# Zero products on TensorE ahead of the first weights, and another order of the first tiles' steps, in a graph attention layer with a spline network

## The reference

```python
HW = h @ W
s = HW @ a[:OUT_F, 0]
t = HW @ a[OUT_F:, 0]
e = jax.nn.leaky_relu(s[row] + t[col], negative_slope=ALPHA)
m = jax.ops.segment_max(e, row, num_segments=N_NODES)
ex = jnp.exp(e - m[row])
den = jax.ops.segment_sum(ex, row, num_segments=N_NODES)
agg = jax.ops.segment_sum((ex / den[row])[:, None] * h[col], row, num_segments=N_NODES)
basis = _b_splines(agg, _grid())
out = jax.nn.silu(agg) @ base_w.T + jnp.einsum('nip,oip->no', basis, spline_w)
return _layernorm(x + out, axis=-1)
```

## Time and profile before

| | before |
|---|---|
| median of 3 runs | 412.33 us |
| the profiled execution | 412.93 us |
| its span, first to last instruction | 411.1 us |
| TensorE busy | 378.2 us (92%) |
| VectorE busy | 353.7 us (86%) |
| ScalarE busy | 261.5 us (64%) |
| mean granted TensorE clock | 0.973 |

### The profile page before, as it was taken

How to read it: one execution, slowest core, us unless ns; L and a number is a source line. 1 busy time by engine, 2 the same in 40 slices (tenths; PEclk the granted TensorE clock), 3 DMA queues, 4 the chain that set the end, 5 groups by cost and what they waited for, 6 DMA issues and landing times.

```text
span 411.1 us, 5022 instructions
## 1 busy us (share of the span) xinstructions
PE 378.2 (92%) x1850; PEld 295.6 (72%) x1850; DVE 353.7 (86%) x442; ACT 261.5 (64%) x264; POOL 32.8 (8%) x108
## 2 busy tenths in 40 slices
PE   5997615999999999899999999999999999999993
PEld 2545404888888888778788888788777777777782
DVE  7999959977887587999899999989799959999645
ACT  2758427465665697886587686496476677678212
POOL 5100001000000000010101010101010010101000
PEclk9999865999999999999999999999999999999999
DMA  7996826000000009545364545442524164563202
GB/s 258 385 236 20 28 17 206 0 2 0 0 2 0 2 4 348 183 123 186 107 200 139 169 129 178 121 136 56 150 53 102 51 176 158 135 192 83 71 18 105
DMA packets 23882, 46.54 MB, mean 113 GB/s; under 512 B 1878, under 2 KB 2218, under 8 KB 23858
## 3 DMA queue, kind: packets, MB, share of 16 engines
q1 hardware_dynamic: 12770, 24.78, 22.9%
q0 software_dynamic: 11088, 21.44, 19.2%
HBM read 43.02 MB, written 2.56 MB: 111 GB/s over the span
## 4 chain that ended last, share of the span: by engine, by line
PE 50%; issue 31%; DVE 11%; POOL 4%; DMA 2%; DVEq 1%; ACT 0%; POOLq 0%
PE PS L1165 25%; PE PS L1121 17%; POOL wh L410 3%; DVE oh L419 3%; PE PS L1104 3%; DMA wh<-in_splT 2%; PE PS L1067 2%; DVE still L433 2%; PE PS L1131 1%; PE PS L1032 1%; DVE xl L442 1%; DVE wl L642 1%; PE PS L1053 0%; DVE ex L678 0%; DVE scrap L650 0%
## 5 line engine op out<-in xcount | busy, mean ns | idle before, releaser
L1165 PE MATMUL PS<-wh,s 128*128 128x512 f32 (+1 forms) x720 | 225.3, 392 | 2.2 <-DVE wl L642 1.0
L1165 PEld LDWEIGHTS PS<-wh,s 128*128 128x128 f32 (+1 forms) x720 | 133.4, 185 | 36.5 <-ACT s L935 3.7
L1165 PE MATMUL PS<-wl,s 128*128 128x512 f32 (+1 forms) x360 | 141.1, 392 | 0.0
L935 ACT ACTIVATE s<-v 128x1280 fp32r<-128x1280 f32 (+1 forms) x32 | 40.0, 1252 | 63.9 <-DVE v L750 59.4
L1165 PEld LDWEIGHTS PS<-wl,s 128*128 128x128 f32 (+1 forms) x360 | 66.7, 185 | 15.2
L744 DVE SCALAR_TENSOR_TENSOR v<-v,v 128x1280 f32<-128x1280 f32 (+1 forms) x32 | 46.5, 1454 | 4.8 <-ACT v L921 4.8
L750 DVE SCALAR_TENSOR_TENSOR v<-v,v 128x1280 f32<-128x1280 f32 (+1 forms) x32 | 46.7, 1461 | 3.3
L760 DVE SCALAR_TENSOR_TENSOR s<-v,s 128x1280 fp32r<-128x1280 f32 (+1 forms) x32 | 46.5, 1454 | 0.2 <-ACT s L935 0.2
L746 DVE SCALAR_TENSOR_TENSOR v<-v,v 128x1280 f32<-128x1280 f32 (+1 forms) x32 | 46.5, 1454 | 0.0
L918 ACT ACTIVATE v<-xt,bias 128x1280 f32<-128x1280 f32 (+1 forms) x32 | 42.9, 1342 | 3.5 <-DVE s L760 2.1
L410 POOL DMA_DIRECT2D wh<-in_splT x32 | 22.9, 714 | 279.1 <-PE PS L1165 164.2
(11 more groups left out here) (133 smaller groups left out, 353.4 us busy)
## 6 DMA issues: line engine op xcount, KB each, us to landing
wh<-in_splT POOLq DMA_DIRECT2D x32, 512.0 KB, 4.8
wring<-in_splT SPq DMA_DIRECT2D x21, 512.0 KB, 4.3
xt<-in_xT SPq DMA_DIRECT2D x1, 2500.0 KB, 11.6
xn<-in_x SPq DMA_DIRECT2D x1, 2304.0 KB
xh<-in_x POOLq DMA_DIRECT2D x1, 2304.0 KB, 13.3
out<-xr SPq DMA_DIRECT2D x9, 256.0 KB
wh<-in_baseT POOLq DMA_DIRECT2D x4, 512.0 KB, 4.8
wring<-in_baseT SPq DMA_DIRECT2D x3, 512.0 KB, 4.2
```

The costliest lines, as they stand in the source:

```text
L935: e.activation(parts(sh, u), bufs(u)[0], ACT.Relu).then_inc(s_shi, 1)
L1165: m = e.matmul(PS[0:rows(w), w % 8, :], sx[:, ic, tl * 128:tl * 128 + rows(w)], wx[:, ic, :], start=first and n == 0, stop=last and n == 2)
```

## The change

`keep_warm(n)` issues `n` products of a zero matrix with 500 zero columns into PSUM bank 6, and nothing reads them. Eight stand ahead of the loop over the remaining edges, six behind it, eight more behind a wait for `greatest(0)`, four behind `e1(0, 0)`, four behind `e2(0, 0)`; then comes the first transpose. The order of steps for tiles 0 to 3 changes on VectorE, ScalarE and TensorE.

```diff
@@ vector
             greatest(0)
             small(0)
             greatest(1)
+            weigh(0, 0)
             small(1)
-            weigh(0, 0)
             weigh(0, 1)
-            inverse(0)
             p_low(0, 0)
+            weigh(1)
             greatest(2)
             small(2)
             p_low(0, 1)
-            weigh(1)
+            inverse(0)
             inverse(1)
+            greatest(3)
+            p_low(1)
             weigh(2)
             inverse(2)
-            p_low(1)
-            greatest(3)
             small(3)
             greatest(4)
             small(4)
@@ scalar
             for p in range(2):
                 e1(0, p)
                 e2(0, p)
+            p_high(0, 0)
             e1(1)
-            p_high(0, 0)
+            e2(1)
             p_high(0, 1)
-            e2(1)
             e1(2)
+            p_high(1)
             e2(2)
-            p_high(1)
             normalise(0)
             e1(3)
-            e2(3)
             for j in range(1, NT - 1):
...
                 p_high(j + 1)
+                if j == 1:
+                    e2(3)
@@ tensor
+            def keep_warm(n):
+                for k in range(n):
+                    e.matmul(PS[:, 6, 0:CW], nought[:, 0:128], nought[:, :], start=True, stop=True)
+
             e.wait_ge(s_scol, 3)
+            keep_warm(8)
             with e.Fori(0, left) as n:
...
-            def aggregate(j, i0=0, i1=3):
-                if j >= 2 and i0 == 0:
+            def aggregate(j, products):
+                end = 1 if j == 0 else 2
+                if j >= 2 and 0 in products:
                     e.wait_ge(s_ya, j - 1)
-                for i in range(i0, i1):
+                for i in products:
...
-                    if j <= 1 and i == 2:
+                    if j == 0 and i == 2:
                         e.wait_ge(s_xlo, NT)
...
+            keep_warm(6)
+            e.wait_ge(s_tmax, 1)
+            keep_warm(8)
+            e.wait_ge(s_e1, 1)
+            keep_warm(4)
+            e.wait_ge(s_e2, 1)
+            keep_warm(4)
             turn(0, 0)
             turn(0, 1)
-            for j in range(NT):
-                aggregate(j, 0, 2)
+            aggregate(0, (0, 2))
+            turn(1)
+            aggregate(0, (1,))
+            for j in range(1, NT):
+                aggregate(j, (0, 1))
                 if j + 1 < NT:
                     turn(j + 1)
-                aggregate(j, 2, 3)
-                if j:
-                    back(j - 1)
+                aggregate(j, (2,))
+                back(j - 1)
```

More of the change, by code:

```diff
@@ L1121, in aggregate @@
                         m = e.matmul(PS[:, 5 + j % 2, :], pp[0:r, j % 3, place(j, t), :], xs[0:r, t, :],
-                                     start=(i == 0 and t == 0), stop=(i == 2 and t == NT - 1))
-                if i1 == 3:
+                                     start=(i == 0 and t == 0), stop=(i == end and t == NT - 1))
+                if end in products:
                     m.then_inc(s_agg, 1)
```

## The result

Over 17 runs of each the changed kernel takes 413.33 us against 412.14 us: a ratio of 1.0029 (95% interval 1.0019 to 1.0039). The runs spread more, 412.04 to 414.94 us against 411.56 to 412.7 us. Forecast was 412.1 us and no change; the range 411.0 to 413.5 us holds the time, the direction is wrong. Ratios leave out an execution that is over 1.5% above the fastest of its kernel; the only one in this document is the 421.98 us of `after_256`.

A forecast was written before the change was run, and what follows sets the result against it. VectorE's and ScalarE's queues, not TensorE's clock, were taken as the bound. -0.55 (new order) + 0.2 (first eight) + 0.05 (clock) = -0.3, taken as -0.25: 412.33 - 0.25 = 412.1 us, range 411.0 to 413.5.

The forecast's parts named there:

- `weigh(1)` behind `e2(1)`: VectorE's `weigh(1)` waits for ScalarE's `e2(1)` and starts near 68.9 us, which hides `p_low(0, 0)`.
- the gap in `turn(1)` and its releaser: TensorE waits almost 1 us before the ninth transpose of `turn(1)`, until VectorE's L701, `p_low(0, 1)`, is done.
- the last group of tile 0: TensorE's last products of tile 0 start near 75.2 us, where before they started at 75.55.
- the gain there: Attention stage: 0.55 us gained, 0.2 lost to the first eight and 0.05 to the clock: 0.3, taken as 0.25.
- the first eight: Zero products ahead of the loop's product L1089: at half clock they end at 57.95 and make it 0.2 us late.
- the prediction's own bound: The eight at full clock take 1.7 us, end by 56.3, cost nothing; a faster L1089 gives back up to 0.2.
- the sixteen: Zero products behind `greatest(0)`: 3.4 us at full clock, over by 64.7, not holding up the first transpose.
- the 0.1 that the prediction had weighed: If transposes don't count as busy, the clock is lost before tile 0's 20 products; the gain is 0.1 us smaller.
- So 0.55 is kept, and the stage goes on as before: Tile 0's last group starts at 75.0 instead of 75.55 us; later steps of tiles 1 to 3 keep that lead.
- its signs of being wrong: `turn(0, 0)` coming after 65.5 us, no gap in `turn(1)`, or TensorE waiting anew at `turn(2)`.
- the rivals: TensorE bounded after all, 411.0 us, chance 0.17; zero products in the way; first eight at upper bound, 413.7 us, 0.03.
- the slower one: Sixteen zero products before `turn(0, 0)`, half of them at half clock: +1.2 us, 413.5 us; chance 0.23 in all.

The follow-up runs named there:

- `after_256`: Changed kernel plus 196 do-nothing TensorE instructions (satisfied waits) in the first stage and around the loop: 418.0 us, ratio 1.0138 to the kernel before.
- `zeros_only`: Kernel before, in its own order of steps, with the 30 zero products added: 413.49 us, ratio 1.0031.
- `early_low`: Changed kernel with seven zero products ahead of the loop, earlier `p_low(0, 1)` and `p_high(1)`, and 198 satisfied waits in tiles 2 to 8: 411.74 us, ratio 0.9986.
- the changed kernel plus 196: Changed kernel with 196 do-nothing TensorE instructions (satisfied waits) spread over the products of tiles 2 to 8: 412.0 us, ratio 0.9994 to the kernel before.
- 30 waits: Kernel before with 30 satisfied waits on TensorE spread over products: 412.99 us, ratio 1.002.
- 120: Kernel before with 120 satisfied waits on TensorE spread over the products of tiles 2 to 6: 412.48 us, ratio 1.0006.

## Why the prediction was wrong

Right, by its own steps: where the bound stood (VectorE's queue, not the clock; `zeros_only` shows it for the old order), `weigh(1)` behind `e2(1)` (68.9 said, 68.91 measured), the gap in `turn(1)` and its releaser (almost 1 us said, 0.76 by the sum, 0.90 measured), the last group of tile 0 (75.2 said, 75.20 measured), the gain there (0.25 to 0.3 said, 0.36 measured).

Right in number alone, and so by luck: the first eight, with 0.2 us taken and 0.26 measured. At half clock they were to hold the loop's product until 57.95. In fact the clock fell at 55.3 us, with four of them under way at full clock; they ended at 57.22, TensorE idled 0.71 us, and VectorE's operand was there at 57.54, as before (57.52). In `zeros_only` the eight ran at full clock, were over at 56.4, and the product still came 0.30 us late, where the prediction's own bound had no delay. Between the start of L618 and that product lie 0.47 us in the kernel before and in `early_low` with seven, 0.71 and 0.72 in the changed kernel and `zeros_only`, 0.57 in the changed kernel plus 196. What holds it up is open.

Missed, at little cost: the clock was to be back before 61 us and came at 62.2, after two of the sixteen had run at half. The last of them started at 64.91 us and the first transpose's load of weights at 65.02, released by VectorE's L681 at 64.97; so they held it up by 0.1 us at most. Nor does the clock stay for certain: it lasted in the profiles of the changed kernel and `zeros_only`, and was at 0.50 again from 67.3 to 70.7 us in the changed kernel plus 196 and from 68.3 to 71.7 in `early_low`. There `turn(2)` started at 82.06 (plus 196) against 81.97 us: the 0.1 that the prediction had weighed.

Wrong is the sentence in which the sum was closed, "So 0.55 is kept, and the stage goes on as before", with its counterpart "from 80 us on everything as before, 0.3 us earlier". It priced the added products as work in an idle stretch and left out that they are 60 instructions in a stream that is fetched in blocks. None of its signs of being wrong could show it, since all of them end by 82 us. The omitted term is a fetch one unit earlier: in the profiled execution 1.6 us of idle time near 204 us; by medians 1.2 us over the kernel before, or 1.5 us over the changed kernel's own attention stage. Removing it by moving the fetch a whole period (0.9994) and making it without the change (1.0025, 1.0033) both work, so the shift of the code is shown to be the cause; that it costs by late loads is read from the profiles, in each of the three that lost time at this place. None of the rivals had it; the slower one named the sixteen zero products in the way, and the timeline excludes that (0.1 us at most, with the first transpose at 65.02 for 64.9 said). The result came near its price by accident.

The row that could have warned stood on the page: the code queue, q8, with 15 packets. And the kernel before carries the same effect in its own timeline, VectorE's wait of 1.79 us for a load near 204 us and TensorE's of 0.65 us at 265 us.

Open: why one packet of 16 KB holds one DMA engine back by 2.5 to 3 us. What that engine moved alone in the changed kernel is about 2.5 us at 25 GB/s, some 60 KB; its share of the two loads is 2 x 512 / 16 = 64 KB. That looks as if it began both only when the others were done, but no run here tells it from other ways. With 30 waits the loss was 0.2% where none was expected, with 120 none clear of noise where 0.2 to 0.35% was expected; one profile each doesn't explain it. Nor is it settled why the same place is hit in some executions and not in others.

## What to carry to other kernels

Instructions that only fill idle time still shift every later code fetch of their engine; where loads are timed tightly, count the added instructions and compare, in the trace, the code packets with the issue times of the loads. A slower or faster ratio of 0.3% after an edit that shouldn't matter later can be tested with do-nothing instructions: as many as the edit added should reproduce it in the old kernel, and a full period should undo it in the new one. They must stand where they hold nothing up, since each took 0.11 us here when they stood in a row. And a late load costs only where the engine that consumes it has no slack behind it, so a place with slack is where a fetch should fall.

## What was not expected of the hardware

- A code packet that starts as two loads of 512 KB are issued can leave one DMA engine working alone at 18 to 27 GB/s for 2 us or more (an estimate from the rate); the loads then land after 6.7 to 8.1 us instead of 4.2 to 5.4. In `early_low` a packet 0.65 us behind the first issue instead of 0.55 did nothing of the kind.
- Code fetches of TensorE stand near the start of a unit whether 30 or 60 instructions are added (190.1 and 189.8 us), not half a unit apart.
- A wait that is already satisfied isn't free on TensorE's sequencer: 49 instructions of two waits each took from 51.2 to 56.4 us in `after_256`, 0.11 us apiece.
- The register load L229 on TensorE took 0.49 us when it began at 56.6 us and 3.08 to 3.29 us when it began near 51.3 us; what it waits for in the latter, no run shows.
